# A three-phase transformer kernel: the short last chunk of the second feed-forward layer stacked in halves, and two heads' values in one 32-row group

## The chip, the cores and the metric

The kernel runs on one core of one Trainium2 chip. The metric is the device time of one execution in microseconds (us); three runs of the kernel before took 1309.91 to 1316.45 us, with a median of 1315.11 us. Names of engines: PE is TensorE (PEld its weight load), DVE is VectorE, ACT is ScalarE, POOL is GpSimd, SP is SyncE, which issues most of the DMAs.

## The reference, cut to what matters

Input are 2048 tokens, width 256. Three models follow one another, each added to what came before.

```python
h = tok(tokens)                                   # 4 layers: state space + feed-forward
h = h + attn(layernorm(h))                        # 16 heads of width 16
h = h + ffn(layernorm(h))                         # 2 layers: window attention + feed-forward

# attn, per sequence of 256 positions as the kernel runs it (8 of them), H, D = 16, 16
qh, kh, vh = (x @ Wq, x @ Wk, x @ Wv), each in 16 heads
dist   = maximum(|q|^2 - 2 q.k + |k|^2, 0)
scores = where(later key, 0, exp(-gamma * dist / 4))
out    = (scores @ vh), heads side by side, @ Wo

# ffn, one layer: window attention with 8 heads of width 64, then, with HID = 682
a, g = split(norm(shift(x)) @ w1 + b1)
x = x + (a * gelu(g)) @ w2 + b2                   # 682 rows of w2 = 5 chunks of 128 and one of 42
```

All matrix products are fp32 quality: an operand x is kept as hi (rounded to the matmul's own format) and lo = x - hi, and a product takes three matmuls, hi by hi, hi by lo and lo by hi.

## The kernel before, in words

The program is written engine by engine; every dependence is a semaphore, and the order of work on each engine is the order in which its instructions are written out. Nothing is planned at run time: an instruction that waits holds up all that stands behind it on its engine.

**First phase** (`tower_phase`): the token model. Its layers run on groups of 4 tiles of 128 tokens. In layer 0, SP loads the attention weights into `raw` (lines 200 to 205: one DMA each for Wq, Wk and Wv, four for Wo). Wo is loaded in four row groups of 32 rows of which 16 hold data, the rest zeroed by a memset of POOL (line 733). In the last layer ACT makes the hi parts (line 430) and POOL the lo parts (line 728), one of four parts in each step.

**Second phase** (`attention_phase`): 8 steps s of 256 tokens, software-pipelined over several halves. On PE a half runs `project_v`, transposes (line 903), `distances` (lines 916 and 919, 8 pairs of heads), `values` (lines 935 and 933), `project_out` (lines 944 to 946) and `project_qk` (lines 877 to 879). `values(s, q, b)` takes quad q of four heads: head j of the quad has a 32-row group of PSUM, of which the head's 16 value columns fill 16 rows, and the rest are zeros out of `v`'s padding. The four quads lie in four column ranges of 256 tokens, two per PSUM bank. So the output has 4 chunks of 128 rows, half of them zeros, and `project_out` has 2 tiles x 4 chunks x 3 = 24 matmuls of 256 columns per step. ACT copies two chunks at a time to the hi part (`output_hi`, line 1161) and DVE makes the lo part (`output_lo`, line 1316). The distances are clipped by DVE (line 1312), go through exp on ACT (line 1154) and are masked by POOL (line 1453).

**Third phase** (`window_phase`): 16 steps f (2 layers x 8 steps of 256 tokens), again in halves; in one half h the feed-forward of step g = h-6 ends while that of f = h-5 begins and the attention of later steps runs. The pieces of the feed-forward, with their lines:

- `norm` (2230), transposes (1924), `affine` (ACT, 2244 and 2245) writes `nf`, which shares its place with the first two chunks of `gate`, and `nh`; `split_normed` (DVE, 2508) makes `nl`; `hidden_in` (PE, 1937 to 1939), 66 matmuls a step; `gelu` (ACT, 2257, 2253, 2254); `gated` (DVE, 2516; for the short chunk 2513).
- `hidden_hi` (ACT, 2264), `hidden_lo` (POOL, 2711; in the last step DVE, 2521) split each of 6 chunks of the hidden layer, `hidden_out` (PE, 1949 to 1951) multiplies them by w2: 2 tiles x 3 matmuls of 256 columns per chunk, also for the sixth chunk, of whose 128 rows 42 hold data.
- `affine(f)` waits until all six chunks of the step before have been split:

```python
if f >= 1:
    act.wait_ge(S["h_split"], FC * f)      # FC = 6
```

Order in a half that matters here: POOL runs the splits of chunks 3, 4 and 5, then `scale_p` (2706, 2707), then `add_bias` (2725; in layer 1 2727 and 2730). DVE runs `split_normed(f)`, `add_attention` (2473), soft 2, `turned_p`, `inverse_sums` (2458), soft 3, `output_lo` (2469), `turned_p` (2464). ACT runs `affine(f)`, `output_hi`, probabilities, gelu 0 to 5. PE runs `hidden_out` of chunks 4 and 5 near the middle of its half, after `hidden_in` of the gate part. The last steps f = 14 and 15 have no attention beside them, so that their pieces follow one another in a chain.

Of the kernel before, what the change touches and what calls it, by code (L numbers as in the profile page):

```python
# [14 lines left out]
P = 128  # L15
# [4 lines left out]
D = 256  # L20
# [18 lines left out]
def attention_raw(raw):  # L39


    return (raw[:, 0:DC * 3 * D].rearrange("p (c n) -> p c n", c=DC),
            raw[:, DC * 3 * D:DC * 3 * D + 4 * D].rearrange("p (q n) -> p q n", q=4))


def tower_phase(nc, sems, X, dram, raw, wa):
# [12 lines left out]
    with ExitStack() as ctx:  # L59
# [92 lines left out]
        wa_raw, wa_zero, wa_h, wa_l = sem("wa_raw"), sem("wa_zero"), sem("wa_h"), sem("wa_l")  # L152
        wa_parts = [(wa[0][:, c, :], wa[1][:, c, :], raw_w[:, c, :]) for c in range(DC)]
        wa_parts += [(wa[2][:, 2 * c:2 * c + 2, :], wa[3][:, 2 * c:2 * c + 2, :], raw_o[:, 2 * c:2 * c + 2, :]) for c in range(2)]
# [200 lines left out]
        def scalar(act, early):  # L355
# [45 lines left out]
            def step(l, g, front, early=None):  # L401
# [26 lines left out]
                if isinstance(l, int):  # L428
                    act.wait_ge(wa_raw, 16 * 7)
# [247 lines left out]
        def gpsimd(pool, early):  # L677
# [55 lines left out]
            pool.memset(raw_o[:, :, :], 0.0).then_inc(wa_zero, 1)  # L733
# [34 lines left out]
def attention_phase(nc, sems, X, dram, wa, out, raw, qkv, tower):  # L768
# [8 lines left out]
    QUAD, HQ = 4, H // 4  # L777
# [12 lines left out]
    with ExitStack() as ctx:  # L790
# [30 lines left out]
        ot_hi = sb("ot_hi", [P, HQ, STOK], F32R)  # L821
        ot_lo = sb("ot_lo", [P, HQ, STOK], F32R)
# [20 lines left out]
        def qkv_raw(k):  # L843
            return raw[:, k * PART:(k + 1) * PART]

# [20 lines left out]
        def tensor(pe):  # L866
# [55 lines left out]
            def values(s, q, b):  # L922
# [3 lines left out]
                t0 = s % 2 * ST  # L926
                for late in range(2):
                    for j in range(QUAD):
                        h = QUAD * q + j
                        slot = h % SLOTS  # L930
                        dst = ps[32 * j:32 * j + 32, 2 * b + q // 2, (q % 2) * STOK:(q % 2 + 1) * STOK]
                        if late:
                            mm = pe.matmul(dst[:, 0:P], v[:, t0, h, :], e[:, slot, 2 * P:3 * P], start=False, stop=True, skip_group_check=True)
                        else:
                            pe.matmul(dst, v[:, t0 + 1, h, :], e[:, slot, 0:2 * P], start=True, stop=False, skip_group_check=True)
                mm.then_inc(pv_done, 1)

            def project_out(s, b):
                pe.wait_ge(ot_split, 2 * s + 2)
                for t in range(ST):  # L940
                    dst = ps[:, 2 * b, t * D:(t + 1) * D]
                    tok = slice(t * P, (t + 1) * P)
                    for q in range(HQ):
                        pe.matmul(dst, ot_hi[:, q, tok], wo_hi[:, q, :], start=(t == 0 and q == 0), stop=False, skip_group_check=True)
                        pe.matmul(dst, ot_hi[:, q, tok], wo_lo[:, q, :], start=False, stop=False, skip_group_check=True)
                        mm = pe.matmul(dst, ot_lo[:, q, tok], wo_hi[:, q, :], start=False, stop=(t == ST - 1 and q == HQ - 1), skip_group_check=True)
# [2015 lines left out]
```

## Time and profile before

| what | us |
|---|---|
| median of three runs | 1315.11 |
| lowest and highest | 1309.91, 1316.45 |
| the profiled execution: device time | 1310.7 |
| its span in the profile | 1308.9 |
| PE busy | 1232.5 (94%) |
| DVE busy | 974.7 (74%) |
| ACT busy | 865.2 (66%) |
| POOL busy | 631.1 (48%) |

The busy share of an engine over the whole span is an average over three phases; the first ends at about 525 us, the second at about 690 us, where it overlaps the start of the third. The mean granted TensorE clock is 0.986 of full speed. A busy PE is not a PE at its peak. A matmul's duration is longer than its share of the engine, since matmuls overlap; the distance between two starts is what one of them costs.

### The profile page before, as it was taken

What the parts mean: (1) busy time and instruction counts of PE and PEld (TensorE: products, weight loads), DVE (VectorE), ACT (ScalarE), POOL (GpSimd) and SP (SyncE); (2) the same over time, 40 slices, a digit from 0 to 9 for tenths busy, and PEclk for the clock granted to TensorE, in tenths of its full rate; (3) what the DMA queues carried; (4) which work ended last, traced back from release to release, by engine and by line L of the source; (5) the groups of instructions that cost most, each with busy time, mean ns of one, the idle gap of its engine ahead of it and who ended that gap; (6) DMA issues with size and microseconds to landing.
All of it is one profiled execution on the core that took longest, in us unless ns stands there. A gap on an engine that the chain in (4) does not pass through costs nothing.

```text
span 1308.9 us, 26308 instructions
## 1 busy us (share of the span) xinstructions
PE 1232.5 (94%) x9027; PEld 1053.2 (80%) x9027; DVE 974.7 (74%) x2609; ACT 865.2 (66%) x1987; POOL 631.1 (48%) x694
## 2 busy tenths in 40 slices
PE   5899999999999999899977899999999999999997
PEld 4799889889988988677765667888888887888886
DVE  5767676676667777899878988878787888777633
ACT  2455766675566555789865568778777777777743
POOL 7423441351145343455235567556556666566442
PEclk9899999999999999899999899999999999999998
DMA  7300010010000000210010002000100000000000
GB/s 168 111 2 15 2 64 0 14 54 10 0 8 1 1 1 29 46 47 17 17 53 17 1 5 91 5 5 6 48 5 7 17 4 14 21 22 21 22 22 21
DMA packets 35489, 33.19 MB, mean 25 GB/s; under 512 B 12474, under 2 KB 32050, under 8 KB 35378
## 3 DMA queue, kind: packets, MB, share of 16 engines
q1 hardware_dynamic: 34482, 29.65, 7.5%
q0 software_dynamic: 768, 2.10, 1.0%
q8 instruction: 61, 1.00, 0.3%
q14 instruction: 50, 0.41, 0.1%
q10 hardware_dynamic: 128, 0.04, 0.0%
HBM read 25.75 MB, written 4.19 MB: 23 GB/s over the span
## 4 chain that ended last, share of the span: by engine, by line
PE 45%; DVE 6%; issue 3%; ACT 3%; POOL 3%; DVEq 0%; ACTq 0%; POOLq 0%
PE w_ring L1937 3%; PE w_ps_p L1877 3%; PE w_ring L1938 3%; PE w_ring L1939 3%; PE w_ring L1836 3%; PE w_ring L1838 3%; PE w_ring L1837 3%; PE w_ps_a L1895 2%; PE w_ring L1949 2%; PE a_ps L903 2%; PE w_ps_d L1870 2%; PE w_ps_d L1867 2%; PE w_ring L1854 2%; PE w_ring L1950 1%; PE w_ring L1951 1%
## 5 line engine op out<-in xcount | busy, mean ns | idle before, releaser
L377 ACT ACTIVATE t_gf<-t_ps_f,t_fb_cur 128x512 f32<-128x512 f32 x128 | 87.9, 687 | 170.5 <-PE t_ps_f L283 167.3
L296 PE MATMUL t_ps_o<-t_w_hi,t_g_hi 128*128 128x256 f32 x512 | 146.4, 286 | 3.2 <-DVE t_g_lo L527 3.1
L527 DVE TENSOR_TENSOR t_g_lo<-t_gf,t_g_hi 128x512 fp32r<-128x512 f32 x128 | 94.0, 736 | 70.7 <-ACT t_g_hi L379 69.7
L298 PE MATMUL t_ps_o<-t_w_hi,t_g_lo 128*128 128x256 f32 x512 | 145.2, 284 | 0.0
L297 PE MATMUL t_ps_o<-t_w_lo,t_g_hi 128*128 128x256 f32 x512 | 145.1, 283 | 0.0
L680 POOL TENSOR_TENSOR t_rs<-t_ve,t_neghalf 128x4 f32<-128x4 f32 x32 | 37.5, 1173 | 168.7 <-DVE t_ve L488 167.3
L1937 PE MATMUL w_ring<-w_nh,w_w_hi 128*128 128x256 f32 x352 | 105.1, 299 | 6.8 <-DVE w_nl L2508 5.0
L2464 DVE COPY w_pt<-w_ps_p 128x384 f32<-128x384 f32 x128 | 70.5, 551 | 53.1 <-PE w_ps_p L1877 51.5
L296 PEld LDWEIGHTS t_ps_o<-t_w_hi,t_g_hi 128*128 128x128 f32 x512 | 98.0, 191 | 7.7 <-issue 4.3
L2695 POOL TENSOR_TENSOR w_m<-w_m 128x512 f32<-128x512 f32 x64 | 85.5, 1335 | 38.9 <-DVE w_m L2421 38.8
L281 PE MATMUL t_ps_f<-t_nh,t_w_hi 128*128 128x512 f32 x256 | 102.9, 402 | 1.3 <-DVE t_nl L503 0.8
L282 PE MATMUL t_ps_f<-t_nh,t_w_lo 128*128 128x512 f32 x256 | 101.2, 395 | 0.0
L297 PEld LDWEIGHTS t_ps_o<-t_w_lo,t_g_hi 128*128 128x128 f32 x512 | 98.2, 192 | 2.4
L283 PE MATMUL t_ps_f<-t_nl,t_w_hi 128*128 128x512 f32 x256 | 100.1, 391 | 0.0
L1938 PE MATMUL w_ring<-w_nh,w_w_lo 128*128 128x256 f32 x352 | 99.9, 284 | 0.0
L1939 PE MATMUL w_ring<-w_nl,w_w_hi 128*128 128x256 f32 x352 | 99.7, 283 | 0.0
L298 PEld LDWEIGHTS t_ps_o<-t_w_hi,t_g_lo 128*128 128x128 f32 x512 | 98.2, 192 | 0.0
L2711 POOL TENSOR_TENSOR w_h_lo<-w_gate,w_h_hi 128x256 fp32r<-128x256 f32 x90 | 65.2, 736 | 51.7 <-ACT w_h_hi L2264 51.4
L1836 PE MATMUL w_ring<-qkv_hi,w_ah 128*128 128x512 f32 x188 | 80.7, 429 | 6.1 <-DVE w_al L2403 4.8
L379 ACT ACTIVATE t_g_hi<-t_gf 128x512 fp32r<-128x512 f32 x128 | 80.9, 632 | 4.0
L2706 POOL TENSOR_TENSOR w_pr<-w_pr,w_rinv 128x256 f32<-128x256 f32 x64 | 39.3, 614 | 87.5 <-DVE w_rinv L2458 87.5
L1154 ACT ACTIVATE a_e<-a_dist,a_gsc 128x384 f32<-128x384 f32 x128 | 70.3, 622 | 12.3 <-DVE a_dist L1312 10.8
(317 smaller groups left out, 4311.1 us busy)
## 6 DMA issues: line engine op xcount, KB each, us to landing
t_raw<-in_L_tok_w SPq DMA_DIRECT2D x8, 1024.0 KB, 5.3
out<-X SPq DMA_DIRECT2D x14, 256.0 KB, 2.1
raw<-in_L_ffn_wqkv SPq DMA_DIRECT2D x2, 1536.0 KB, 6.5
raw<-in_L_ffn_w SPq DMA_DIRECT2D x4, 640.0 KB, 5.3
w_raw_o<-out SPq DMA_DIRECT2D x8, 256.0 KB, 2.7
w_xs<-X SPq DMA_DIRECT2D x14, 127.0 KB
w_raw<-in_L_ffn_w SPq DMA_DIRECT2D x2, 640.0 KB
t_raw_d<-in_L_tok_D SPq DMA_DIRECT2D x4, 256.0 KB, 3.0
```

The costliest lines, as they stand in the source:

```text
L281: pe.matmul(ps_f[:, j % 2, :], w1_hi[:, c, col], nh[1][:, c, :], start=(c == 0), stop=False)
L282: pe.matmul(ps_f[:, j % 2, :], w1_lo[:, c, col], nh[1][:, c, :], start=False, stop=False)
L283: mm = pe.matmul(ps_f[:, j % 2, :], w1_hi[:, c, col], nl[1][:, c, :], start=False, stop=(c == DC - 1))
L296: pe.matmul(out, g_hi[:, j % 4, tok], w2_hi[:, j, :], start=(j == 0 and t % 2 == 0), stop=False, skip_group_check=True)
L297: pe.matmul(out, g_hi[:, j % 4, tok], w2_lo[:, j, :], start=False, stop=False, skip_group_check=True)
L298: mm = pe.matmul(out, g_lo[:, j % 4, tok], w2_hi[:, j, :], start=False, stop=(j == FC - 1 and t % 2 == 1), skip_group_check=True)
L377: act.activation(gf[:, j % 2, :], ps_f[:, j % 2, :], ACT.Gelu, bias=fb_cur[:, j:j + 1]).then_inc(pf_free, 1)
L527: dve.tensor_tensor(g_lo[:, j % 4, :], gf[:, j % 2, :], g_hi[:, j % 4, :].bitcast(F32), ALU.subtract).then_inc(g_split, 1)
L1836: pe.matmul(ring[:, RB[b], :], ah[:, c, tok], qkv_hi[:, c, cols], start=(c == 0), stop=False)
L1937: pe.matmul(dst, w1_hi[:, c, u, cols], nh[:, c, :], start=(j % 2 == 0 and c == 0), stop=False, skip_group_check=True)
L1938: pe.matmul(dst, w1_lo[:, c, u, cols], nh[:, c, :], start=False, stop=False, skip_group_check=True)
L1939: mm = pe.matmul(dst, w1_hi[:, c, u, cols], nl[:, c, :], start=False, stop=(j == chunks[-1] and c == DC - 1), skip_group_check=True)
```

## The change

Second phase. The two quads that share a PSUM bank now add into the same 256 columns: quad (o, y) puts its heads' 16 values into rows 16y to 16y+15 of the 32-row groups, and the other 16 columns of `v` are zeros. The columns of Wv and the rows of Wo are permuted as they are loaded, so that the order of heads fits. The output has 2 chunks of 128 full rows; `ot_hi`, `ot_lo` and the parts of Wo are half as large; `output_hi` and `output_lo` handle 256 columns each. In the first phase this takes 8 DMAs for Wv with runs of 16 elements at the target, and 8 for Wo; the memset of POOL and SP's wait for it go.

Third phase. The hi part of the sixth chunk lies in rows 0 to 41 of its slot of `h_hi`, its lo part in rows 64 to 105 of the same slot, and w2's last 42 rows are held twice in `w2_hi`. Two matmuls a tile instead of three. The lo part is made by DVE instead of POOL, after soft 3, behind a wait for the first five splits; `affine` waits for the first two splits of the step before only, and gelu of chunk 2 waits for all six. w2's last rows are loaded by one more DMA and copied by one more ACT instruction in each layer.

```diff
-                    for i, name in enumerate(("L0_attn_Wq", "L0_attn_Wk", "L0_attn_Wv")):
+                    for i, name in enumerate(("L0_attn_Wq", "L0_attn_Wk")):
                         sp.dma_start(raw_w[:, :, D * i:D * i + D], ...).then_inc(wa_raw, 16)
-                    sp.wait_ge(wa_zero, 1)
-                    wo = dram["L0_attn_Wo"].rearrange("(q j d) n -> j d q n", j=4, d=16)
-                    for j in range(4):
-                        sp.dma_start(raw_o[32 * j:32 * j + 16, :, :], wo[j]).then_inc(wa_raw, 16)
+                    wv = dram["L0_attn_Wv"].rearrange("(c p) (o y j d) -> c o y p j d", p=P, y=2, j=4, d=16)
+                    for c in range(DC):
+                        raw_v = raw_w[:, c, 2 * D:3 * D].rearrange("p (o j y d) -> p o y j d", j=4, y=2, d=16)
+                        for o in range(2):
+                            for y in range(2):
+                                sp.dma_start(raw_v[:, o, y, :, :], wv[c, o, y]).then_inc(wa_raw, 16)
+                    wo = dram["L0_attn_Wo"].rearrange("(o y j d) n -> y j d o n", y=2, j=4, d=16)
+                    for y in range(2):
+                        for j in range(4):
+                            sp.dma_start(raw_o[32 * j + 16 * y:32 * j + 16 * y + 16, :, :], wo[y, j]).then_inc(wa_raw, 16)
...
-            pool.memset(raw_o[:, :, :], 0.0).then_inc(wa_zero, 1)
...
             def values(s, q, b):
-                        dst = ps[32 * j:32 * j + 32, 2 * b + q // 2, (q % 2) * STOK:(q % 2 + 1) * STOK]
+                        dst = ps[32 * j:32 * j + 32, 2 * b + o, 0:STOK]
+                        vh = 2 * (QUAD * o + j) + y
                         if late:
-                            mm = pe.matmul(dst[:, 0:P], v[:, t0, h, :], e[...], start=False, stop=True, ...)
+                            mm = pe.matmul(dst[:, 0:P], v[:, t0, vh, :], e[...], start=False, stop=(y == 1), ...)
                         else:
-                            pe.matmul(dst, v[:, t0 + 1, h, :], e[...], start=True, stop=False, ...)
+                            pe.matmul(dst, v[:, t0 + 1, vh, :], e[...], start=(y == 0), stop=False, ...)
...
             def project_out(s, b):
-                    for q in range(HQ):
+                    for q in range(HO):
...
-                act.activation(ot_hi[:, 2 * k:2 * k + 2, :]..., ps[:, 2 * b + k, :], ACT.Copy).then_inc(ot_h, 1)
+                act.activation(ot_hi[:, k, :], ps[:, 2 * b + k, 0:STOK], ACT.Copy).then_inc(ot_h, 1)
...
+                for row in (0, UP):
+                    sp.dma_start(raw_2[row:row + LAST, FC - 1, :], w2[(FC - 1) * P:HID, :]).then_inc(S["raw_2"], 16)
...
             def hidden_out(f, j, b):
                     pe.matmul(dst, h_hi[:, j % HS, tok], w2_hi[:, j, :], ...)
-                    pe.matmul(dst, h_hi[:, j % HS, tok], w2_lo[:, j, :], start=False, stop=False, ...)
-                    mm = pe.matmul(dst, h_lo[:, j % HS, tok], w2_hi[:, j, :], start=False, stop=(j == FC - 1 and t == ST - 1), ...)
+                    mm = pe.matmul(dst, h_hi[:, j % HS, tok], w2_lo[:, j, :], start=False, stop=(j == FC - 1 and t == ST - 1), ...)
+                    if j == FC - 1:
+                        continue
+                    mm = pe.matmul(dst, h_lo[:, j % HS, tok], w2_hi[:, j, :], start=False, stop=False, ...)
...
             def hi_2(l):
+                for row in (0, UP):
+                    act.activation(w2_hi[row:row + LAST, FC - 1, :], raw_2[row:row + LAST, FC - 1, :], ACT.Copy)
...
             def affine(f, p):
-                    act.wait_ge(S["h_split"], FC * f)
+                    act.wait_ge(S["h_split"], FC * f - FC + DC)
...
             def gelu(f, j, b):
+                if f and j == DC:
+                    act.wait_ge(S["h_split"], FC * f)
...
             def hidden_lo(f, j):                                   # DVE
                 dve.wait_ge(S["h_hi"], FC * f + j + 1)
+                if j == FC - 1:
+                    dve.wait_ge(S["h_split"], FC * f + j)
+                    dve.tensor_tensor(h_hi[UP:UP + LAST, j % HS, :], gate[0:LAST, j, :], h_hi[0:LAST, j % HS, :].bitcast(F32), ALU.subtract).then_inc(S["h_split"], 1)
+                    return
...
                     soft(H * c + 3)                                # DVE half
+                if 0 <= g < M - 1:
+                    hidden_lo(g, 5)
...
                     hidden_lo(f, 4)                                # POOL half
-                    hidden_lo(f, 5)
```

## Rows read from the trace of the kernel before

**Rows 1.** Busy time by stage: length, PE, PEld, DVE, ACT, POOL, clock, DMA share, GB/s

```profile
577.00:595.60 18.60, 18.46 (x181) 14.45 (x181) 17.95 (x42) 17.32 (x37) 10.83 (x14) 1.00 0.05 16
...
614.20:632.80 18.60, 18.46 (x181) 14.45 (x181) 16.12 (x35) 16.80 (x35) 8.86 (x12) 1.00 0.05 16
...
934.70:970.60 35.90, 35.90 (x276) 30.54 (x278) 28.61 (x91) 26.27 (x75) 20.30 (x23) 1.00 0.02 5
...
1286.70:1292.60 5.90, 5.90 (x28) 5.90 (x29) 0.00 (x0) 1.29 (x4) 0.00 (x0) 0.51 0.00 0
```

**Rows 2.** Chain that ended last, one output projection (second, last matmul): start, us

```profile
623.03 0.12 PE a_ps L945
...
625.60 0.11 PE a_ps L946
```

**Rows 3.** Groups by line, DVE and ACT: count, busy us, mean ns, idle before

```profile
L1316 DVE TENSOR_TENSOR a_ot_lo<-a_ps,a_ot_hi 128x512 fp32r<-128x512 f32 x16 | 10.9, 683 | 1.7 <-ACT a_ot_hi L1161 1.6
...
L2469 DVE TENSOR_TENSOR w_ot_lo<-w_ps_a,w_ot_hi 128x256 fp32r<-128x256 f32 x64 | 26.5, 414 | 1.6 <-ACT w_ot_hi L2224 1.4
...
L2513 DVE TENSOR_TENSOR w_gate<-w_last_a,w_gate 42x256 f32<-42x256 f32 x16 | 7.0, 436 | 0.0
...
L1161 ACT ACTIVATE a_ot_hi<-a_ps 128x512 fp32r<-128x512 f32 x16 | 9.5, 593 | 1.2 <-PE a_ps L933 0.5 <-PE a_ps L946 0.3
...
L2224 ACT ACTIVATE w_ot_hi<-w_ps_a 128x256 fp32r<-128x256 f32 x64 | 24.5, 383 | 52.6 <-PE w_ps_a L1893 52.2
```

**Rows 4.** Chain that ended last, end of the second phase: start, us

```profile
679.33 0.61 ACT a_ot_hi L1161
```

**Rows 5.** Timeline, DVE, POOL, ACT, one third-phase half without stalls: start, us

```profile
974.39 0.42 DVE L2469 TENSOR_TENSOR w_ot_lo<-w_ps_a,w_ot_hi 128x256 fp32r<-128x256 f32 x1
977.39 0.56 DVE L2464 COPY w_pt<-w_ps_p 128x384 f32<-128x384 f32 x1 [2.58 <-PE w_ps_p L1877]
...
974.42 1.04 POOL L2707 TENSOR_TENSOR w_pr<-w_pr,w_rinv 128x512 f32<-128x512 f32 x1
...
976.98 1.93 ACT L2257 ACTIVATE w_gate<-w_ring,w_b_all 128x256 f32<-128x256 f32 x5
```

**Rows 6.** Timeline, a split on DVE, a weight split on POOL: start, us

```profile
896.06 2.87 DVE L2508 TENSOR_TENSOR w_nl<-w_gate,w_nh 128x512 fp32r<-128x512 f32 x1 [0.82 <-ACT w_nh L2245]
...
895.99 2.38 POOL L2690 TENSOR_TENSOR qkv_lo<-raw,qkv_hi 128x1024 fp32r<-128x1024 f32 x1
```

**Rows 7.** Chain that ended last, step f = 15: start, us

```profile
1281.76 1.65 issue
...
1285.37 1.14 DVE w_nl L2508
...
1286.65 0.55 PE w_ring L1937
```

**Rows 8.** Timeline, POOL at f = 15, PE at f = 14: start, us

```profile
1281.23 2.10 POOL L2711 TENSOR_TENSOR w_h_lo<-w_gate,w_h_hi 128x256 fp32r<-128x256 f32 x3 [1.42 <-ACT w_h_hi L2264]
1283.29 1.26 POOL L2727 TENSOR_TENSOR X<-X,w_b_all 128x512 f32<-128x512 f32 x1
...
1267.54 0.36 PE L1937 MATMUL w_ring<-w_nh,w_w_hi 128*128 128x256 f32 x1 [0.90 <-DVE w_nl L2508]
```

**Rows 9.** PE's waits, 840 us to the end: total us, times, longest us

```profile
PE w_ring L1937 <- DVE w_nl L2508: 5.0, 3, 3.7
```

**Rows 10.** Two other stalls of PE: timeline row, then stages (columns of Rows 1)

```profile
1237.02 0.55 PE L1877 MATMUL w_ps_p<-w_ident,w_pr 128*128 128x128 f32 x3 [2.09 <-POOL w_pr L2707]
...
1238.00:1241.00 3.00, 3.00 (x17) 2.58 (x14) 1.41 (x6) 1.05 (x3) 0.00 (x0) 0.50 0.00 0
...
564.40:566.50 2.10, 0.00 (x1) 0.00 (x1) 2.07 (x4) 0.03 (x2) 1.48 (x2) 1.00 0.44 28
```

**Rows 11.** DMA of Wv: KB, us to landing; its use: ns min/median/max, first start

```profile
raw<-in_L_attn_Wv SPq DMA_DIRECT2D x1, 256.0 KB, 3.8
...
L430 ACT ACTIVATE wa_whi<-raw x2: 852/852/852, 431.0 to 460.3; 128x768 fp32r<-128x768 f32 x2
```

More of the change, by code:

```diff
@@ L151, in tower_phase @@
         raw_w, raw_o = attention_raw(raw)
-        wa_raw, wa_zero, wa_h, wa_l = sem("wa_raw"), sem("wa_zero"), sem("wa_h"), sem("wa_l")
+        wa_raw, wa_h, wa_l = sem("wa_raw"), sem("wa_h"), sem("wa_l")
         wa_parts = [(wa[0][:, c, :], wa[1][:, c, :], raw_w[:, c, :]) for c in range(DC)]
-        wa_parts += [(wa[2][:, 2 * c:2 * c + 2, :], wa[3][:, 2 * c:2 * c + 2, :], raw_o[:, 2 * c:2 * c + 2, :]) for c in range(2)]
+        wa_parts += [(wa[2][:, c, :], wa[3][:, c, :], raw_o[:, c, :]) for c in range(DC)]
         def tiles(g):
@@ L942, in project_out @@
                     tok = slice(t * P, (t + 1) * P)
-                    for q in range(HQ):
+                    for q in range(HO):
                         pe.matmul(dst, ot_hi[:, q, tok], wo_hi[:, q, :], start=(t == 0 and q == 0), stop=False, skip_group_check=True)
                         pe.matmul(dst, ot_hi[:, q, tok], wo_lo[:, q, :], start=False, stop=False, skip_group_check=True)
-                        mm = pe.matmul(dst, ot_lo[:, q, tok], wo_hi[:, q, :], start=False, stop=(t == ST - 1 and q == HQ - 1), skip_group_check=True)
+                        mm = pe.matmul(dst, ot_lo[:, q, tok], wo_hi[:, q, :], start=False, stop=(t == ST - 1 and q == HO - 1), skip_group_check=True)
                 mm.then_inc(y_full, 1)
@@ L1128, in keep_values @@
                     act.wait_ge(pv_done, NQUAD * (s - 1))
-                act.activation(v[:, s % 2 * ST + t, :, 0:HD], ps[:, 2 * b, 0:D].rearrange("p (h d) -> p h d", h=H), ACT.Copy).then_inc(v_done, 1)
+                act.activation(value_halves(s % 2 * ST + t), ps[:, 2 * b, 0:D].rearrange("p (g y d) -> p g y d", y=2, d=HD), ACT.Copy).then_inc(v_done, 1)
             def turned_q(s, t, b):
@@ L1160, in output_hi @@
                     act.wait_ge(y_full, s)
-                act.activation(ot_hi[:, 2 * k:2 * k + 2, :].rearrange("p q t -> p (q t)"), ps[:, 2 * b + k, :], ACT.Copy).then_inc(ot_h, 1)
+                act.activation(ot_hi[:, k, :], ps[:, 2 * b + k, 0:STOK], ACT.Copy).then_inc(ot_h, 1)
             def qkv_first(k):
@@ L1210, in first_kept @@
                 act.wait_ge(v_full, 2)
-                act.activation(v[:, t, :, 0:HD], ps[:, 1, t * D:(t + 1) * D].rearrange("p (h d) -> p h d", h=H), ACT.Copy).then_inc(v_done, 1)
+                act.activation(value_halves(t), ps[:, 1, t * D:(t + 1) * D].rearrange("p (g y d) -> p g y d", y=2, d=HD), ACT.Copy).then_inc(v_done, 1)
             def opening(j):
@@ L1949, in hidden_out @@
                     pe.matmul(dst, h_hi[:, j % HS, tok], w2_hi[:, j, :], start=(j == 0 and t == 0), stop=False, skip_group_check=True)
-                    pe.matmul(dst, h_hi[:, j % HS, tok], w2_lo[:, j, :], start=False, stop=False, skip_group_check=True)
-                    mm = pe.matmul(dst, h_lo[:, j % HS, tok], w2_hi[:, j, :], start=False, stop=(j == FC - 1 and t == ST - 1), skip_group_check=True)
+                    mm = pe.matmul(dst, h_hi[:, j % HS, tok], w2_lo[:, j, :], start=False, stop=(j == FC - 1 and t == ST - 1), skip_group_check=True)
+                    if j == FC - 1:
+                        continue
+                    mm = pe.matmul(dst, h_lo[:, j % HS, tok], w2_hi[:, j, :], start=False, stop=False, skip_group_check=True)
                 mm.then_inc(S["h_used"], 1)
@@ L2147, in hi_2 @@
             def hi_2(l):
[L2148 removed]
+                act.wait_ge(S["raw_2"], 48 * l + 48)
                 act.wait_ge(S["h_used"], NSQ * FC * l)
                 act.wait_ge(S["fill"], 2)
[L2151 removed]
+                for row in (0, UP):
+                    act.activation(w2_hi[row:row + LAST, FC - 1, :], raw_2[row:row + LAST, FC - 1, :], ACT.Copy)
                 act.activation(w2_hi[:, 0:FC - 1, :], raw_2[:, 0:FC - 1, :], ACT.Copy).then_inc(S["hi_2"], 1)
@@ L2263, in hidden_hi @@
                     act.wait_ge(S["h_used"], FC * f + j - HS + 1)
-                act.activation(h_hi[:, j % HS, :], gate[:, j, :], ACT.Copy).then_inc(S["h_hi"], 1)
+                rows = LAST if j == FC - 1 else P
+                act.activation(h_hi[0:rows, j % HS, :], gate[0:rows, j, :], ACT.Copy).then_inc(S["h_hi"], 1)
             def half(h):
@@ L2835, in program @@
             wa = [first.enter_context(nc.sbuf_tensor(f"wa_{x}", [P, n, w], F32R))
-                  for n, w, k in ((DC, 3 * D, "w"), (4, D, "o")) for x in (k + "hi", k + "lo")]
+                  for n, w, k in ((DC, 3 * D, "w"), (DC, D, "o")) for x in (k + "hi", k + "lo")]
             tower_sems, sems = [], []
```

25 lines of the change are left out of this document (12 added, 13 removed).

## The prediction

> **What bounds the kernel now.** I read the busy time by stage first, then the chain that ended last, then the groups by line, and timelines where a stage stalls. In the busy time by stage [rows 1] the reader is to see that PE fills 18.46 of 18.60 us in a steady step of the second phase and all of 35.90 us in a steady half of the third. So a matmul taken out there shortens the kernel, as long as nobody else is close. In the third phase nobody is (DVE 28.61, ACT 26.27). In the second phase both are: DVE 17.95 and ACT 17.32 of 18.60 in the early step, 16.12 and 16.80 in the later one. The last steps of the third phase are another stage: a chain through all engines, in which PE waits, and behind the longest wait its granted clock is 0.51, the lower level of 1.2 GHz.
>
> **Part 1, the output projection of the second phase.** A step has 24 matmuls of 256 columns. From the second to the last, 22 distances lie between 623.03 and 625.60 us [rows 2]: 0.117 us each. Twelve go: 12 x 0.117 = 1.40 us of PE per step, in 8 steps. ACT and DVE lose half of two copies and two subtractions. By the copies of 256 columns that the third phase already has [rows 3], 2 x (0.593 - 0.383) = 0.42 us of ACT and 2 x (0.683 - 0.414) = 0.54 us of DVE per step. The matmuls of `values` stay in number and columns, so they cost what they cost.
>
> What is late next: with PE at 18.60 - 1.40 = 17.20 us, DVE needs 17.95 - 0.54 = 17.41 us in the early step, and ACT 16.90 us plus the small gaps between some 35 instructions. In the later step both are below 16.4. The engines are coupled at several points of a step, PE waits for the values' copy, and exp and mask run in step with it, so that I do not take the full 1.40. By kinds of step:
> - step 0, where PE still waits for DVE: 0.8 us; ends 0.5 (DVE's part) and 1.4.
> - steps 1 to 4: 1.1 us each, 4.4; ends 0.5 each, 2.0, if the bound passes to DVE or ACT, and 5.6.
> - step 5, in front of the run-out of DVE's clips: 1.4; ends 0.5 and 1.9.
> - step 6, where the chain is in DVE's clips and the next phase's norm: 0; ends 0 and 0.3.
> - step 7, the last: its copy is on the chain itself [rows 4], followed by the subtraction and the projection: 1.40 + 0.21 + 0.27 = 1.9; ends 1.4 and 1.9.
>
> Together 8.5 us, ends 4.4 and 11.1.
>
> **Part 2, the stacked chunk.** Two matmuls fewer in each of 16 steps, of the same shape: 32 x 0.117 = 3.7 us. All stand in PE's full halves or in the chain at the end; the lower end is 3.0, if a few fall beside a stall.
>
> The lo part moves from POOL to DVE. There it is 42x256 with two inputs from SBUF, like the product of line 2513: 0.44 us [rows 3], 15 times. In a steady half it stands where `output_lo` starts now, at 974.39, and DVE's next instruction is waited for until 977.39, with 2.58 us idle [rows 5]. That idle time covers it: price 0. Behind it queue `output_lo`, a copy of transposed probabilities and two more softmax pieces; if the cover were gone, PE would wait for these. It also waits for POOL's fifth split, which in a steady half is done well before: POOL is already at `scale_p`, two operations on [rows 5]. The new wait of ACT, before gelu of chunk 2, has its margin in the same rows: gelu starts at 976.98.
>
> A rule against this part: the split on DVE can be held up by POOL. The row shows the case: `split_normed` took 2.87 us beside a weight split of 2.38 us on POOL [rows 6], where it took 1.14 us in the last step [rows 7]. At 974.42 POOL has an operation of 1.04 us [rows 5]; the new split would end at about 975.9 and `output_lo` at 976.3, still before 977.39. So the price stays 0 in steady halves; I keep 1.0 us for all halves in which POOL splits weights, as the bad end. The Trainium skill, GPSIMD Engine Reference, section Key points, says the same as a rule: POOL shares its SBUF interfaces with DVE, and contention arises with DVE instructions of two SBUF inputs, as the new one is. The trace agrees, with the 2.87 us; were the rule to bite for POOL's whole 1.04 us in each of 15 halves without cover, the sum would be 15 us worse, as in the first rival that ends without a gain.
>
> **Part 3, the relaxed wait.** At f = 15, ACT stands idle for 1.65 us before `affine` [rows 7], while POOL does three splits from 1281.23 to 1283.33 [rows 8]. The new wait is for the first two splits, long done, so `affine` moves up by 1.65. `split_normed` follows its start by 1285.37 - 1283.41 = 1.96 us [rows 7], so it starts near 1283.7, and may wait for POOL's bias addition [rows 8], which itself moves up by a split of 0.70 us; it takes up to 1.1, and ends near 1284.8 instead of 1286.5. PE waits 3.7 us there [rows 9], so it gains the whole: 1.8. At f = 14 the same happens, but PE has other work and waits only 0.90 us [rows 8]: gain 0.9. Together 2.7; lower end 0.9, if POOL's additions hold DVE up.
>
> **Part 4, the clock.** Behind the 3.7 us wait, 28 matmuls take 5.90 us at a granted clock of 0.51 [rows 1]; at 0.117 us they would take 3.3. So the wait costs another 2.6 us. With some 2.0 us left of it, the traces have both outcomes [rows 10]: after a wait of 2.09 us the clock was at 0.50 for over 3 us, cost about 1.6; after 2.1 us without a matmul elsewhere it stayed at 1.00. I take the nearer stage, 2.6 - 1.6 = 1.0; ends 0 and 2.6.
>
> **Part 5, the rest.** One more ACT copy of 42 rows per layer, like a 256-column copy [rows 3]: 2 x 0.4, mostly beside PE's work; I take 0.2, ends 0 and 0.8. The copies of v write the same number of elements in another pattern: 0. Eleven more DMAs in the first phase, those of Wv in short runs. Were each of the 8 as slow as the whole Wv now, 3.8 us, they would take 30 us one after another, and the weights are first read at 431.0 us [rows 11]. SP's next loads are for layer 1, tens of us away from their use. Price 0; if the cover were gone, the start of layer 1 would be late by what exceeds it. The halved parts of Wo end with POOL's last split of the first phase, and PE's last transposes end later than that: 0, upper end 0.7.
>
> **Sum:** 8.5 + 3.7 + 2.7 + 1.0 - 0.2 = 15.7 us. The profiled execution took 1310.7: 1295.0. It lies 4.4 below the median of the three runs, 1315.11; against the median the sum gives 1299.4. I forecast 1299. Worst ends: 4.4 + 3.0 + 0.9 + 0 - 0.8 - 1.0 = 6.5; best 11.1 + 3.7 + 2.7 + 2.6 + 0.7 = 20.8.
>
> **Rivals.**
> - *The second phase passes to DVE and ACT.* For it: 17.95 and 17.32 of 18.60 in the early steps. Against: DVE has 2.5 and ACT 1.8 us idle in the later ones [rows 1]. Then steps 0 to 5 give 0.5 each: 3.0 + 1.9 = 4.9 instead of 8.5, and the time is 1303.
> - *Everything PE loses is won, and the clock holds.* 11.1 + 3.7 + 2.7 + 2.6 = 20.1: 1295. For it: PE is gapless; against: three engines near their limit.
> - *The new split holds DVE up behind POOL.* Price 1.0 us in each of 15 halves, 15 in all; from the point at which the split comes after POOL's operation and the 2.58 us are used up. Then what is left is within the noise: 1314.
> - *Slower: ACT's new wait before gelu of chunk 2.* Six halves have a long weight split on POOL, and `split_normed` there takes up to 2.87 us [rows 6]. If the lo part lands after gelu 1, ACT stands, and behind it the table load, the probabilities and, through `gated`, PE's `hidden_out`. It decides from 1.9 us of lateness against [rows 5]; to end slower, each of these halves must lose 4 us: 24 - 15.7, 1323. Against: no row shows the split's inputs that late.
> - *It doesn't do what it says.* The loop counts make the matmuls fewer for certain; that none of it shows is in the third rival.
>
> **How the numbers follow.** Forecast 0.55, DVE and ACT 0.22, all won 0.12, split behind POOL 0.08, slower 0.03. The range takes in the second and the first rival and the spread of the bounds, and is widened since single runs of this kernel lie 6.5 us apart: 1289 to 1308. About 0.5%, 6.6 us, is what a measurement can tell from no change; the first three cases are faster than that: 0.89, 0.08, 0.03.
>
> **What would show it right or wrong.** 12 matmuls of lines 944 to 946 per step, and a steady step of the second phase of 17.2 to 17.6 us instead of 18.60, with PE still full; if 18.1 or more, the first rival. A steady third-phase half of 35.67 us. DVE's new instruction at 0.4 to 1.5 us with `turned_p` behind it still waiting for PE. ACT's idle 1.65 us before `affine` gone, PE's longest wait on line 1937 near 2.0 instead of 3.7, and the clock behind it. A wait of gelu on `h_split`, or of PE on DVE's copies in a steady half, would prove the prediction wrong; so would a step of the second phase unchanged at 18.60.

## The result, and the profile after

The changed kernel takes 1296.07 us (median of 4 runs, 1295.72 to 1297.33), the kernel before, run beside it, 1315.78 (4 runs, 1309.91 to 1317.43). The ratio is 0.9872, with a 95% interval from 0.9847 to 0.9897: faster by 1.3%. The profiled executions took 1295.74 and 1310.7 us, 15.0 apart. The medians are 19.7 apart because the kernel before has runs near 1310 and runs near 1316, and three of its four were of the second kind here; in 57 further runs of it, beside the experiments, the medians were 1310.1 to 1310.7. In 6 further runs the kernel after had a median of 1295.1. So the change is worth 15 us between like runs.

Busy time by stage of the kernel after, for the stretches that answer to those of [rows 1] (length, PE, PEld, DVE, ACT, POOL, clock, DMA share, GB/s):

```profile
577.76:595.43 17.67, 17.16 (x169) 13.03 (x169) 17.29 (x42) 16.70 (x37) 10.84 (x14) 1.00 0.06 17
613.08:630.27 17.19, 17.06 (x168) 13.03 (x168) 15.75 (x35) 16.12 (x35) 8.87 (x12) 1.00 0.05 17
917.68:953.35 35.67, 35.67 (x274) 30.31 (x274) 29.67 (x92) 26.27 (x75) 19.14 (x21) 1.00 0.06 17
1275.00:1279.00 4.00, 4.00 (x36) 4.00 (x35) 0.88 (x1) 1.68 (x4) 0.60 (x1) 1.00 0.00 0
```

The early step has gone from 18.60 to 17.67 us and its DVE is busy 17.29 of it; the later step is at 17.19 with PE full, the whole 1.40 us won. The steady half of the third phase is 35.67 instead of 35.90. Behind the longest wait of the tail the clock is 1.00, where it was 0.51.

The groups by line of the kernel after that answer to [rows 3], with the new split of 42 rows:

```profile
L1326 DVE TENSOR_TENSOR a_ot_lo<-a_ps,a_ot_hi 128x256 fp32r<-128x256 f32 x16 | 6.6, 415 | 3.7 <-ACT a_ot_hi L1171 3.7
L2539 DVE TENSOR_TENSOR w_h_hi<-w_gate,w_h_hi 42x256 fp32r<-42x256 f32 x16 | 16.3, 1017 | 0.7 <-ACT w_h_hi L2280 0.3
...
L1171 ACT ACTIVATE a_ot_hi<-a_ps 128x256 fp32r<-128x256 f32 x16 | 6.0, 375 | 2.4 <-PE a_ps L943 2.2
```

The copies and subtractions of the output cost what [rows 3] say for 256 columns. The new split takes 1.02 us on average and not 0.44, as it stands beside POOL's work.

The chain that ended last in the tail of the kernel after, f = 15 (start, us), against [rows 7]:

```profile
1271.09 0.71 ACT w_h_hi L2280 x2
1271.81 0.46 ACT w_gate L2257
...
1273.66 0.80 DVE w_nl L2524
1274.46 0.14 issue
1274.60 0.36 PE w_ring L1947
```

ACT's 1.65 us of idle time before `affine` are gone, and the norm's split takes 0.80 instead of 1.14 us. PE's waits from 831 us to the end (total us, times, longest), against [rows 9]:

```profile
PE w_ps_p L1887 <- POOL w_pr L2729: 4.7, 4, 2.1
...
PE w_ring L1947 <- DVE w_nl L2524: 1.6, 1, 1.6
```

Where the time went, by the starts of the same instruction in traces (us). "Second alone" and "third alone" are two experiments below; the turn of x of step s is PE's group of four transposes in the second phase, line 871 before; `add_output` is DVE's addition that ends a step f of the third phase.

| | before | after | second alone | third alone |
|---|---|---|---|---|
| turn of x, s = 2 | 538.38 | 538.60 | 538.19 | 539.00 |
| s = 3 | 556.13 | 557.72 | 555.80 | 559.30 |
| s = 4 | 576.99 | 577.76 | 575.85 | 581.64 |
| s = 7 | 632.76 | 630.27 | 628.34 | 637.44 |
| first `add_output`, f = 0 | 834.28 | 829.01 | 829.49 | 838.92 |
| twelfth `add_output`, f = 11 | 1228.46 | 1219.95 | 1223.72 | 1229.96 |
| that of f = 14 | 1295.26 | 1280.36 | 1289.42 | 1290.12 |
| the last, f = 15 | 1304.29 | 1289.18 | 1298.47 | 1298.93 |

From the first to the last `add_output` the kernel after needs 460.17 us where the kernel before needed 470.01: 9.8 us come from the third phase, and 5.3 from all that is ahead of it.

### The profile page after: what moved, and what is told of

It is laid out like the page before. It is cut to its first block, busy times and chain, and to the rows that moved or that the text cites. A ratio compares the mean times of both kernels' runs of the same rounds, so it can differ in the third digit from the quotient of the medians.

```text
span 1293.8 us, 26097 instructions
## 1 busy us (share of the span) xinstructions
PE 1218.6 (94%) x8899; PEld 1035.8 (80%) x8899; DVE 988.7 (76%) x2624; ACT 860.9 (67%) x1989; POOL 618.5 (48%) x678
## 4 chain that ended last, share of the span: by engine, by line
PE 45%; DVE 6%; ACT 3%; POOL 3%; issue 3%; DVEq 0%; ACTq 0%; POOLq 0%
PE w_ps_p L1887 3%; PE w_ring L1947 3%; PE w_ring L1948 3%; PE w_ring L1949 3%; PE w_ring L1846 3%; PE w_ring L1848 3%; PE w_ring L1847 3%; PE w_ps_a L1905 2%; PE a_ps L911 2%; PE w_ring L1959 2%; PE w_ps_d L1880 2%; PE w_ps_d L1877 2%; PE w_ring L1864 2%; PE w_ring L1960 2%; PE w_ring L1963 1%
## 5 line engine op out<-in xcount | busy, mean ns | idle before, releaser
L2717 POOL TENSOR_TENSOR w_m<-w_m 128x512 f32<-128x512 f32 x64 | 84.2, 1316 | 37.5 <-DVE w_m L2437 37.2
L2733 POOL TENSOR_TENSOR w_h_lo<-w_gate,w_h_hi 128x256 fp32r<-128x256 f32 x75 | 54.5, 736 | 49.1 <-ACT w_h_hi L2280 49.1
```

## The experiments

Twelve kernels ran, each beside the kernel before, whose median in the three groups was 1310.69, 1310.14 and 1310.68 us.

**The two phases apart.** `e1` has the edits of `load_ow`, `hidden_out`, `hi_2`, `affine`, `gelu`, `hidden_hi`, `hidden_lo` and their places; `e2` has all others of the diff.

> The kernel before with only the edits of the third phase: stacked last chunk, its split on DVE, and the relaxed wait of affine. My theory, from the two traces: the third phase lost 9.9 us (start of its steady halves to the last output, 490.06 before, 480.12 after), of them 3.8 in 32 matmuls, 1.1 at f = 14, 4.7 at f = 15 with a clock that holds, 0.4 elsewhere; so this kernel takes 9.9 us less than the kernel before, about 1300.8 by the profiled execution's scale, and the second phase's anchors stay. Rival: the gain at the end came only because the whole kernel was earlier or the clock's state happened to differ; then about 3.7 + 2.7 = 6.4 less. Rival two: the edits of the second phase carry the larger part (12 or more of the 19.7 us between the medians), and this kernel gains at most 7.

> The kernel before with only the edits of the second phase and its weights' loads: values of two heads in one group, output projection in two chunks. My theory: 5.2 to 6.7 us less (5.2 is what the second phase gave between the two traces, 1.5 of a clock drop at 549 us may or may not come again); the third phase unchanged, with its wait of 3.7 us on line 1937 and a granted clock near 0.5 behind it. Rival: the 8.5 us of my prediction are there, since step 7 gives its 1.9 us when the third phase doesn't change: 8.5 less. Steps 1 and 2 at 17.6 to 17.8, steps 3 to 6 at 17.2.

Third phase alone: 1301.34 us, ratio 0.9919 (0.9899 to 0.9940); its third phase took 460.01 us. The expected 9.9 are there in the trace (470.01 - 460.01 = 10.0; 9.35 by the medians), and the first rival, 6.4, is out. Second phase alone: 1304.12, ratio 0.9942 (0.9922 to 0.9962), 6.6 less by the medians, inside the 5.2 to 6.7. PE's waits in the second kernel from 831 us on:

```profile
PE w_ring L1946 <- DVE w_nl L2517: 5.2, 3, 3.7
```

The 3.7 us are still there. The clock fell behind them too, but for half as long as in the kernel before: the tail from f = 13's `add_output` to f = 14's took 19.77 us instead of 21.15. 9.35 + 6.57 = 15.9: within the spread of these runs the two halves of the change add up to the 15 of the whole, and no large part is shared between them.

**The relaxed wait alone.** The kernel before with:

```
-  act.wait_ge(S["h_split"], FC * f)
+  act.wait_ge(S["h_split"], FC * f - FC + DC)
...
+  if f and j == DC:
+      act.wait_ge(S["h_split"], FC * f)
```

> The kernel before with only the relaxed wait: affine waits for the first two splits of the hidden rows, gelu of chunk 2 for all; the last chunk's six matmuls and its split on POOL stay. My theory: the relaxed wait alone gives the whole end effect, 1.8 us at f = 15, 0.9 at f = 14 and 2.6 of the clock that then holds: 5.3 less, and no window of 1 us behind f = 15 at a clock below 0.9. Rival: the clock falls all the same, as the wait of some 2 us is as long as the one at 1237 us: 2.7 less, clock near 0.5 in two or three windows. Rival two: the wait that is moved to gelu of chunk 2 gives it back: 0 to 1 less.

1305.70 us (12 runs), ratio 0.9964 (0.9944 to 0.9984): 5.0 less by the medians, near the expected 5.3. The profiled execution (1314.52 us) shows the first rival's case and not the theory's: its tail from the twelfth `add_output` to the last gained 3.3 us (2.7 were that rival's), since there the clock did fall. Its waits of PE, its chain and its stage behind the wait:

```profile
PE w_ring L1937 <- DVE w_nl L2510: 2.7, 2, 2.3
```

```profile
1290.01 1.49 DVE w_nl L2510
```

```profile
1292.00:1295.00 3.00, 3.00 (x16) 3.00 (x15) 0.00 (x0) 0.56 (x2) 0.62 (x1) 0.50 0.00 0
```

DVE's split took 1.49 us here and 0.80 in the kernel after, where one of POOL's three splits has gone to DVE. The stacked chunk so seems to help the tail beyond its matmuls; by which of POOL's operations was not tried. The wait moved to gelu of chunk 2 cost nothing.

**The clock alone.** The kernel before, with its waits, and 28 idle matmuls ahead of `hidden_in(f, 0, 1, 3, "g_full")` at f = 15:

```
+  if f == M - 1:
+      pe.wait_ge(S["pt_done"], H * M)
+      for i in range(28):
+          pe.matmul(ps_p[:, 0, 0:D], ot_hi[:, i % IC, 0:P], wo_hi[:, i % IC, :], start=True, stop=True, ...)
```

> The kernel before with 28 idle matmuls of 256 columns (their result is read by nobody) in front of the matmuls of chunk 0 in every... in the one step f = 15 in which PE waits 3.7 us; nothing else is changed, the wait neither. 28 x 0.117 = 3.3 us fit into the 3.7 us. Theory: the low clock behind that wait costs 2.6 us by itself, so this kernel takes 2.6 us less with the same waits of ACT and DVE, and the clock is 1.00 behind it. Rival: the low clock there is not caused by PE's own idle time; then it stays near 0.5 and the time stays within 0.5 us. Rival two: the extra matmuls push the real ones back, 0.5 to 1 us slower.

1308.24 us (12 runs), ratio 0.9982 (0.9965 to 0.9998): 2.45 less. Its timeline of PE, and the stage behind:

```profile
1283.27 3.46 PE L2069 MATMUL w_ps_p<-w_wo_hi,w_ot_hi 128*128 128x256 f32 x28
1287.07 0.38 PE L1937 MATMUL w_ring<-w_nh,w_w_hi 128*128 128x256 f32 x1 [0.34 <-DVE w_nl L2512]
```

```profile
1288.00:1294.00 6.00, 5.15 (x44) 4.94 (x43) 0.69 (x1) 2.98 (x7) 0.00 (x0) 1.00 0.00 0
```

The norm's split still ends when it did, the wait is only filled, and from the twelfth `add_output` to the last the kernel takes 73.34 us instead of 75.83: 2.5 less, with nothing but work for PE added. The low clock behind the wait cost 2.5 us by itself, as Part 4 worked out. That is the price in this pair of profiles. In the two other profiles with the same wait of 3.7 us the tail from f = 13's `add_output` to f = 14's took 20.68 and 19.77 us, against 21.15 in the kernel before and 18.52 here, so that the low clock cost some 2.2 and 1.2 us there.

**The cover of the new split.** The kernel after with 4 or 8 idle subtractions of 32x256 ahead of it, in 15 halves:

```
   dve.wait_ge(S["h_split"], FC * f + j)
+  free = [...]                                   # four row groups of 32 that nobody reads
+  for i in range(4 if f < M - 1 else 0):
+      ...                                        # a wait for the group of four before
+      dve.tensor_tensor(free[i % 4], gate[0:32, j, :], h_hi[0:32, j % HS, :].bitcast(F32), ALU.subtract)
```

> The kernel after with 4 idle subtractions of 32x256 in front of the new split of 42x256 on DVE, in each of 15 halves. At 0.44 us each (a product of the same size took that) DVE is busy 1.76 us longer in each. Theory: the idle 2.58 us of DVE behind it cover the split and these four (2.2 us), so a steady half stays at 35.67 us or loses up to 0.1, and the time stays within 1.5 us of the kernel after. Rival: the split's own 0.44 us is already on the path somewhere; then each half loses 0.4 to 1.8 us, 6 to 26 in all.

> The same with 8 idle subtractions: 3.5 us and the split, 3.96 us against an idle time of 2.58. Theory: the cover is used up, and of the 1.4 us beyond it PE sees 1.0 to 1.5 in each of 15 halves: a steady half of 36.7 to 37.2 us, 15 to 22 us slower than the kernel after; the chain then passes through these subtractions. Rival: what DVE does next is not waited for so soon, and the half stays below 36.0.

With 4: 1296.59 us. With 8: 1315.74 (12 runs), ratio 1.0036 (1.0022 to 1.0049). A steady half of the first, and one of the second:

```profile
940.58:976.25 35.67, 35.67 (x275) 30.30 (x272) 31.70 (x98) 26.30 (x76) 19.16 (x22) 1.00 0.02 5
```

```profile
947.12:984.24 37.12, 35.86 (x276) 30.33 (x272) 33.32 (x101) 26.41 (x76) 19.16 (x22) 1.00 0.02 5
```

35.67 again, though DVE is busy 2 us longer; and 37.12 with 8, 1.45 us more per half, some 20 us in all. Not every half is as good as the steady ones: with 4, the eleven intervals up to the twelfth `add_output` took 0.5 us more in all (391.47 instead of 390.94). The timeline of DVE with 4 of them:

```profile
970.55 1.67 DVE L2543 TENSOR_TENSOR w_gate<-w_gate,w_h_hi 32x256 f32<-32x256 f32 x2
972.23 0.85 DVE L2543 TENSOR_TENSOR w_last_a<-w_gate,w_h_hi 32x256 f32<-32x256 f32 x2
973.11 0.42 DVE L2546 TENSOR_TENSOR w_h_hi<-w_gate,w_h_hi 42x256 fp32r<-42x256 f32 x1
973.56 0.42 DVE L2485 TENSOR_TENSOR w_ot_lo<-w_ps_a,w_ot_hi 128x256 fp32r<-128x256 f32 x1
973.90 0.55 DVE L2480 COPY w_pt<-w_ps_p 128x384 f32<-128x384 f32 x1
```

The copy follows without idle time: here the cover, 2.58 us in the kernel before, is just used up. The first of the subtractions takes 1.25 us (1.67 for two, where the next two take 0.85), and the split, now later, 0.42: whoever stands first pays for POOL's operation beside it, 0.8 us. In the kernel after that is the split itself, 1.23 us by its median. The third rival was right in its mechanism and near its price (0.8 us against 1.0); the cover pays it.

**POOL's order in the early steps.** In the kernel after the chain runs through POOL in the early steps (chain that ended last: start, us):

```profile
585.41 0.61 ACT a_e L1164
...
586.08 0.64 POOL a_e L1462
586.72 1.27 POOL X L1450
587.99 0.61 POOL a_e L1462
588.60 0.04 issue
588.64 0.40 PE a_ps L945
```

`scale_h` (line 1450) stands between two masks that PE's `values` wait for. It was moved behind the last mask:

```
-  if real(b):
-      scale_h(b)
   if real(f):
       mask(f, 5) ... mask(f, 7)
+  if real(b):
+      scale_h(b)
```

> The kernel after, with POOL's scale_h moved behind the last three masks of a step (after mask 7, before the next step's mask 0). In the steps that start at 577.76 and 595.43 us of the kernel after, the chain runs from exp through the mask, scale_h of 1.27 us and the mask again to the values: with scale_h out of it they should fall from 17.67 and 17.65 to 17.2 to 17.3 us, the later steps stay at 17.2; together 0.8 to 1.0 us less than the kernel after. Rival: DVE (17.29 us busy in the first of them) is the bound and scale_h only stood in time that was idle; then both stay at 17.6 and the time too. Rival two: bias_h and the norm behind scale_h come late, and PE waits at turn_x: 0.5 to 1 us slower.

1297.22 us, ratio 0.9874 (0.9847 to 0.9902): no gain over the kernel after. The two steps took 18.33 and 17.87 us instead of 17.67 and 17.65:

```profile
576.77:595.10 18.33, 17.37 (x171) 13.03 (x169) 18.16 (x43) 17.13 (x37) 10.95 (x14) 1.00 0.05 17
595.10:612.97 17.87, 17.01 (x170) 12.97 (x168) 17.04 (x39) 16.71 (x36) 10.22 (x13) 1.00 0.05 16
```

DVE is busy 18.16 of 18.33, and the chain of this step has hardly anything but DVE beside PE, with one row that tells why:

```profile
590.72 1.38 DVE a_xn L1274
```

The same norm of two tiles in the timelines of the kernel after and of this one:

```profile
591.12 0.75 DVE L1274 TENSOR_SCALAR a_xn<-X,a_mv,a_rs 128x256 f32<-128x256 f32 x2
```

```profile
590.37 1.73 DVE L1274 TENSOR_SCALAR a_xn<-X,a_mv,a_rs 128x256 f32<-128x256 f32 x2
```

POOL's `scale_h` now starts at 590.62, and the norm of DVE beside it takes 1.0 us more. So my theory fell: the chain has passed from POOL to DVE, which had at most 17.67 - 17.29 = 0.38 us to give, and the collision costs more. In the early steps POOL, DVE and PE are all close to the bound.

**The last projection, twice.** Both kernels with `for t in (0, 1, 0, 1) if s == 7 else (0, 1):` in `project_out`: 12 matmuls more in the kernel after, 24 in the kernel before.

> The kernel after, with the output projection of the last step of the second phase done twice (12 matmuls more, 1.4 us of PE; the second pass starts its sums anew). My prediction gave step 7 the whole 1.9 us; the anchors show 0.1. Theory: the last step's end is set by DVE's rotations and softmax pieces of the third phase, not by the projection; then doubling it costs at most 0.4 us, and the first matmuls of the third phase's transposes start at most 0.4 us later against the others. Rival: the chain runs through the projection in the kernel after too, and the 1.4 us show whole at the third phase's first add_output.

> The kernel before with the output projection of the last step of the second phase done twice, 24 matmuls more, 2.8 us of PE at the full clock. My prediction read the projection of the last step as on the chain that sets the end. Theory, after the doubled projection of the kernel after cost nothing: DVE's own queue (norms and rotations of the third phase) is right behind it, so of the 2.8 us at most 1 shows at the third phase's first add_output. Rival: in the kernel before it was on the chain, and 2.3 to 2.8 us show; then the kernel after had lost its gain to the queue behind it.

After, doubled: 1294.62 us, no more than the kernel after (1295.12 in the same group). Before, doubled: 1313.25 (12 runs) against 1310.68, ratio 1.0006 (0.9988 to 1.0024). The medians say 2.6 us, the interval leaves it open, and the traces say more. The addition of the projection to X on DVE, in the kernel before, in its doubled form, in the kernel after and in its doubled form:

```profile
687.42 0.69 DVE L1322 TENSOR_TENSOR X<-a_ps,X 128x512 f32<-128x512 f32 x1 [0.61 <-PE a_ps L946]
```

```profile
693.07 0.69 DVE L1322 TENSOR_TENSOR X<-a_ps,X 128x512 f32<-128x512 f32 x1 [3.09 <-PE a_ps L946]
```

```profile
681.43 0.68 DVE L1331 TENSOR_TENSOR X<-a_ps,X 128x512 f32<-128x512 f32 x1
682.03 1.98 DVE L2413 TENSOR_SCALAR X<-X,w_x_mv,w_x_rs 128x256 f32<-128x256 f32 x4
```

```profile
683.64 0.69 DVE L1331 TENSOR_TENSOR X<-a_ps,X 128x512 f32<-128x512 f32 x1 [0.23 <-PE a_ps L956]
684.25 1.66 DVE L2413 TENSOR_SCALAR X<-X,w_x_mv,w_x_rs 128x256 f32<-128x256 f32 x4
```

In the kernel before DVE waits 0.61 us for the projection; with 2.8 us more of it, 3.09: there it was on the path, by 0.61 us, and 2.5 of the 2.8 us show, as the rival said; my theory of at most 1 fell for the kernel before. In the kernel after DVE doesn't wait: its own queue of rotations reaches the addition last, and 1.4 us more of matmuls cost 0.23, as my theory for it said. The granted clock plays into the 0.61: in the kernel before it was 0.50 from 682 to 684, on PE's matmuls just ahead of the projection. In `e1`, which has the same projection and a clock of 1.00 from 683 on, DVE waits less:

```profile
691.60 0.69 DVE L1322 TENSOR_TENSOR X<-a_ps,X 128x512 f32<-128x512 f32 x1 [0.26 <-PE a_ps L946]
```

So of the 1.40 us taken out, 0.26 to 0.61 could be won. The norm behind the addition took 1.98 us in the kernel after (1.97 or 1.98 in every other profile in which DVE comes to the addition without a wait), against 1.38 in the one before and 1.64 in `e1`. That is as much as was won; that this norm is what took it back was not tried.

**The kernel after again, for the spread.**

> The kernel after as it stands, for the spread. 23 runs of the kernel before gave two clusters, 17 of them 1308.9 to 1312.2 and 6 of them 1314.5 to 1317.3. Theory: both clusters come from the clock, which falls once or twice more in some runs, and each fall costs 1.7 us; the kernel after has a cluster some 5 us up too, in about a quarter of its runs, and its lower one lies at 1294.5 to 1297. Then the gain between like runs is 15, as between the two profiles, not the 19.7 of the medians. Rival: the change removed the upper cluster, and all runs lie within 2 us.

1295.12 us, 1292.78 to 1297.79. Neither theory holds as stated: no cluster 5 us up in 10 runs, and no spread of 2 us either. Its profiled execution took 1292.78 where the first took 1295.74. 1.4 us of the difference lie in the first phase, where the first had a granted clock of 0.57 from 51 to 55 us and this one 1.00 at the same place, and 1.5 in one place of the second: from the turn of x of s = 2 to that of s = 3 17.61 us instead of 19.12. Stages of the one at 1295.74, then of the one at 1292.78, right behind the same stall of PE:

```profile
550.00:553.00 3.00, 3.00 (x21) 2.00 (x14) 2.61 (x7) 2.71 (x7) 1.86 (x4) 0.53 0.00 0
```

```profile
546.00:549.00 3.00, 1.96 (x23) 1.36 (x24) 2.93 (x8) 2.49 (x6) 2.73 (x4) 1.00 0.00 0
```

**A better version.** In the kernel after the longest wait of PE left in the third phase is for POOL's `scale_p`. The timeline of POOL and PE in half 17:

```profile
1225.52 0.54 POOL L2761 TENSOR_SCALAR_AFFINE_SELECT w_m<-w_m 128x128 f32<-128x128 f32 x2
1226.03 0.73 POOL L2733 TENSOR_TENSOR w_h_lo<-w_gate,w_h_hi 128x256 fp32r<-128x256 f32 x1
1226.72 0.61 POOL L2728 TENSOR_TENSOR w_pr<-w_pr,w_rinv 128x256 f32<-128x256 f32 x1
1227.29 1.04 POOL L2729 TENSOR_TENSOR w_pr<-w_pr,w_rinv 128x512 f32<-128x512 f32 x1
...
1228.38 0.65 PE L1887 MATMUL w_ps_p<-w_ident,w_pr 128*128 128x128 f32 x3 [2.10 <-POOL w_pr L2729]
```

`e9` puts `scale_p` ahead of the split and the row matrices behind the next split, on top of the order above; `e10` has this order alone, and 12 idle matmuls in the wait at f = 15.

```
-  if h == M + 1:
-      row_matrices()
+  if h == M + 1:
+      scale_p(NU * c + 2)
   if 0 <= f < M - 1:
       hidden_lo(f, 1)
...
-  if real(c):
+  if real(c) and h != M + 1:
       scale_p(NU * c + 2)
   if 0 <= f < M - 1:
       hidden_lo(f, 2)
+  if h == M + 1:
+      row_matrices()
```

> The kernel after with scale_h moved as in the run before and, in half 17 of the third phase, POOL's scale_p moved ahead of the row matrices and of one split. In the kernel after, PE waits 2.10 us at 1228.38 for scale_p, which started at 1226.72 behind 1.6 us of other work on POOL, and the clock is 0.50 to 0.95 in the four windows from 1229 on. Theory: the wait falls to some 0.5 us (1.6 less) and the clock holds (1.7 less), so 3.3 us less there, and with the 0.9 of scale_h 4.2 less than the kernel after: about 1291.9 and faster than both kernels. Rival: the probabilities are late anyway (exp ends near 1226.5), so only 0 to 0.5 is won; rival two: the moved split is late for PE's hidden_out, which takes back 0.7.

> The kernel after with only the second order of POOL (in half 17 scale_p ahead of one split and of the row matrices) and, in the wait of 1.6 us at f = 15, 12 idle matmuls of 256 columns. With both orders, the stretch from half 17's add_output to the next took 24.97 us instead of 26.46 to 26.68, but the clock fell in the tail in its place (17.7 us from f = 14's add_output to the last split of the norm's end, instead of 16.2) and the first order cost 1.3 us. Theory: 1.6 less from the order, and the filler holds the clock in the tail in all runs: about 2 to 3 us less than the kernel after, 1292 to 1293 median, the best of all. Rival: the filler comes late and delays the real matmuls, or the clock falls elsewhere: no gain over the kernel after.

`e9`: 1296.36 us, ratio 0.9880 (0.9853 to 0.9908). From the twelfth `add_output` to the next it took 24.97 us instead of 26.46, but the tail gave it back. PE's wait at f = 15 is the same 1.6 us as in the kernel after, yet here the clock fell behind it (waits, then stage):

```profile
PE w_ring L1947 <- DVE w_nl L2524: 1.6, 1, 1.6
```

```profile
1272.00:1275.00 3.00, 3.00 (x15) 3.00 (x16) 1.13 (x1) 0.23 (x1) 0.85 (x1) 0.50 0.00 0
```

The record has eight profiles with this wait of 1.6 us at f = 15 and no filler in it, and they are divided. The tail from f = 13's `add_output` to f = 14's took 16.1 to 16.2 us with the clock at 1.00 in four (the kernel after twice, `e1`, and the last projection twice), and 17.6 to 17.7 us with a low clock behind the wait in the other four (`e5`, `e9`, and both kernels with idle subtractions).

`e10`: 1294.91 us (5 runs, 1291.00 to 1297.37), ratio 0.9869 (0.9843 to 0.9895). Its stretch from the twelfth `add_output` to the last is 67.48 us against 69.23 in the kernel after, 1.75 less, and the clock held in the tail. One profile doesn't show that the filler did it, since without a filler the clock held in four of eight. It is the shortest third phase of all, but by the medians it lies 0.8 below the 1295.7 of the ten runs of the kernel after, which these runs can't tell from nothing.

## Why the prediction was right, and where it was not

The forecast was 1299 and the range 1289 to 1308; 1296.07 is in it. The sum gave 1295.0 for the profiled execution, which took 1295.74. The shift of 4.4 us to the median of three runs was what moved the forecast off: that median, 1315.11, lies above those of the 57 further runs of the kernel before (1310.1 to 1310.7), and of ten runs of the kernel after none was above 1297.8.

- **Part 1, 8.5 us; measured 5.3 up to the third phase's first `add_output`.** From the turns of x and the later starts, the step of `project_out` 0 gave 0.82 (I took 0.8), steps 1 and 2 0.94 and 0.93, steps 3 and 4 1.39 each (I took 1.1 for all four: 4.65 against 4.4), steps 5 and 6 together 1.52 (1.4). So far 7.0 against 6.6. Two things take from it. The step that failed is "step 7, the last: its copy is on the chain itself ... 1.9 us; ends 1.4 and 1.9": 0.60 us at the addition, and behind it 0.72 lost again, so net it gave nothing. A copy on the chain says that it binds now, not by how much; the wait of 0.61 us of DVE's addition would have told. And up to the turn of x of s = 3 the profiled execution fell back by 1.6 us, 1.4 of them from s = 2 to s = 3, to a clock that fell there in it and not in the one of before; in the further execution of the kernel after it didn't fall.
- **The bound passing to DVE and ACT.** It passed in the early steps only, to DVE and POOL together. Rival one was right about which steps, but they fell short of the full 1.39 us by 0.46, not by 0.9.
- **Part 2, 3.7 us; measured 3.2** in the first eleven intervals between `add_output`s, 0.23 in each steady one as two matmuls of 0.117 say, and the rest in the tail. One interval gave 0.9 (36.58 us became 35.67): there, in the kernel before, PE waited 0.46 us for the norm's split of 2.87 us [rows 6], and in the kernel after that split took 2.18 and PE didn't wait. The prediction had no term for this. The split takes 1.02 us and not 0.44, and this costs nothing: the runs with 4 and 8 subtractions show the cover at its predicted size. The new wait of gelu was never the last.
- **Part 3, 2.7 us; measured 3.2.** PE's wait went from 3.7 to 1.6 us, 2.1 instead of 1.8 (the prediction's own ends, 1286.5 and 1284.8, give 1.7), as the norm's split also took 0.80 instead of 1.14. At f = 14 the stretch gave 1.30, of which 0.23 are the two matmuls.
- **Part 4, 1.0 us; measured 2.6.** The tail from f = 13's `add_output` to f = 14's gave 4.94 = 2.1 + 0.23 + 2.6: the clock held altogether. The step that was mis-sized is "I take the nearer stage, 2.6 - 1.6 = 1.0". The upper end was right for this execution, and the filler matmuls show the size by themselves. But that the clock held is luck: behind the same wait of 1.6 us it fell in four of eight profiles, which costs 1.5 us (17.6 to 17.7 us against 16.1 to 16.2 for this stretch). With the fall Part 4 would have measured 1.1, about what was forecast.
- **Part 5, 0.2 us.** The second phase's first matmuls behind the first phase start at the same time, 526.09 and 526.12; the eleven DMAs more cost nothing.

The sum was right partly by luck: 3.2 us too many in the second phase stood against 2.4 too few in the third, and 0.2 in Part 5 that did not come.

## What to carry to other kernels

Price a removed instruction on the chain by what its consumer waits for it, not by its own length: 0.61 us was the ceiling for the 1.9 us that I booked, and doubling the work in each kernel showed whether the work was on the path. Where a full engine waits and its clock falls behind the wait, book the wait and the slow stretch as two prices, and try idle matmuls in the wait before rebuilding the queue; here they gave 2.5 us. Whether the clock falls behind a short wait has to be read from several profiles; one of them can show either case. Before an order on a second engine is changed, look at what then runs beside its new place: POOL's operation won nothing where it left and stretched DVE where it arrived.

## What the runs showed of the hardware

The granted clock fell in pieces that cost the same. In all fourteen profiles nearly every fall to 0.50 took 1.7 us of full clock, or a multiple of that, which is the most that it can cost a full PE. By the granted clock over the whole span the kernel before lost 18.5 us of full clock, the kernel after 17.2 and, in its shorter execution, 14.0; where these two executions of the kernel after differed by 2.96 us, 1.4 and 1.5 of it lay at two such falls. Whether a given wait of PE is followed by a fall changed between profiles with the same wait: behind the 1.6 us at f = 15 the clock fell in four of eight, and behind the stall near 547 us it fell by one such piece, by two, or not at all. What decides that was not tried and stays open.

An operation of DVE with two inputs from SBUF was stretched by POOL beside it: the 42x256 split took 1.23 us (median) beside POOL's `scale_p` and 0.42 when four others stood ahead of it and `scale_p` was over. The Trainium skill, GPSIMD Engine Reference, section Key points, says that POOL shares its SBUF interfaces with DVE; the trace agrees, with these two numbers. The norm of line 1274, which reads one tile of X and two columns of factors, was stretched too, from 0.75 to 1.73 us beside `scale_h`.
